# A graph network's message kernel: the first message product of the even quad moved ahead of the rank products

## The reference

```
msg  = concat(x[dst], edge_attr)            # 64 + 64 features per edge
h    = relu(msg @ W1a.T + b1a)              # 128 hidden
h    = h @ W1b.T + b1b                      # 64 per edge: the message
sums = segment_sum(h, src);  counts = segment_sum(1, src)
agg  = sums / max(counts, 1)
z    = relu(concat(x, agg) @ W2a.T + b2a) @ W2b.T + b2b
out  = concat(z, x) @ Wr.T + br
y    = layernorm(x + out)
```

## Time and profile before

| | us |
|---|---|
| median of three runs | 1564.77 |
| span of the profiled execution | 1564.5 |
| PE busy | 1519.9 (97%) |
| PE weight loads busy | 1241.7 (79%) |
| DVE busy | 1400.4 (90%) |
| ACT busy | 1042.4 (67%) |
| POOL busy | 1064.5 (68%) |
| mean granted TensorE clock | 0.990 |

### The profile page before, as it was taken

One profiled execution on the slowest core, in us unless ns is written; L12 is line 12 of the kernel. 1 busy time (PEld: TensorE's weight loads), 2 busy tenths in 40 slices (PEclk: granted clock), 3 DMA queues, 4 the chain that ended last, 5 costly groups with the idle time before them and its releaser, 6 DMA issues.

```text
span 1564.5 us, 42647 instructions
## 1 busy us (share of the span) xinstructions
PE 1519.9 (97%) x13326; PEld 1241.7 (79%) x13326; DVE 1400.4 (90%) x4356; ACT 1042.4 (67%) x2211; POOL 1064.5 (68%) x929
## 2 busy tenths in 40 slices
PE   8999999999999999999999999999999999996897
PEld 6678778778777877877878788888888888875786
DVE  5799999999999999999999999999999999885886
ACT  2587778778787787878877785665556665682222
POOL 2367767677676776767767777778777776876642
PEclk8999999999999999999999999999999999998999
DMA  7556656666565665656656669898999989768997
GB/s 208 166 164 162 177 158 166 170 166 166 159 177 163 164 175 159 167 164 171 165 157 175 174 170 314 261 292 290 294 275 292 293 271 286 230 192 266 367 370 238
DMA packets 135506, 335.44 MB, mean 214 GB/s; under 512 B 36506, under 2 KB 69565, under 8 KB 129016
## 3 DMA queue, kind: packets, MB, share of 16 engines
q0 software_dynamic: 53184, 224.62, 44.4%
q1 hardware_dynamic: 81028, 104.02, 26.3%
q10 hardware_dynamic: 1076, 4.09, 1.0%
HBM read 213.07 MB, written 119.52 MB: 213 GB/s over the span
## 4 chain that ended last, share of the span: by engine, by line
PE 82%; DVE 6%; DMA 3%; POOL 3%; issue 2%; ACT 2%; POOLq 0%; DVEq 0%; ACTq 0%
PE HH L556 21%; PE MS L565 19%; PE PA L581 12%; PE PBk L581 12%; PE RK L594 7%; DMA gbuf<-region,idx 3%; PE RK L674 2%; PE CK L641 2%; PE RK L679 2%; POOL region L1329 2%; PE PA L594 2%; DVE OH L1163 1%; DVE M L1042 1%; POOL gbuf L1357 1%; DVE pos L1047 1%
## 5 line engine op out<-in xcount | busy, mean ns | idle before, releaser
L1329 POOL DMA_INDIRECT region<-stg,dest x806 | 929.4, 1153 | 396.8 <-ACT stg L876 205.6
L565 PE MATMUL MS<-W,hT 128*128 128x64 f32 x3224 | 517.5, 261 | 3.7 <-issue 2.2
L565 PEld LDWEIGHTS MS<-W,hT 128*128 128x128 f32 x3224 | 467.6, 191 | 9.6 <-issue 5.5
L556 PE MATMUL HH<-eab,pw 128*128 128x512 f32 x806 | 433.6, 620 | 1.9 <-ACT hT L825 1.9
L1042 DVE TENSOR_SCALAR M<-pos_of,pos 128x384 bf16<-128x384 int16 x1612 | 427.8, 316 | 0.2
L581 PE MATMUL PA<-Z,M 128*128 128x195 bf16 x2418 | 338.1, 248 | 9.5 <-ACT stg L876 9.0
L581 PE MATMUL PBk<-Z,M 128*128 128x195 bf16 x2418 | 339.1, 248 | 0.0
L581 PEld LDWEIGHTS PA<-Z,M 128*128 128x128 bf16 x2418 | 224.0, 107 | 127.7 <-issue 119.6
L876 ACT ACTIVATE stg<-PA 120x585 bf16<-120x585 f32 x403 | 263.6, 654 | 91.7 <-PE PA L581 86.4
L825 ACT ACTIVATE hT<-HH 128x512 f32<-128x512 f32 x403 | 242.0, 600 | 84.3 <-PE HH L556 84.3
L876 ACT ACTIVATE stg<-PBk 120x585 bf16<-120x585 f32 x403 | 265.4, 659 | 46.2 <-PE PBk L581 44.3
(11 more groups left out here) (213 smaller groups left out, 1516.3 us busy)
## 6 DMA issues: line engine op xcount, KB each, us to landing
eab<-in_ea SPq DMA_DIRECT2D x201, 256.0 KB
kb<-keyd SPq DMA_DIRECT2D x201, 128.0 KB
pw<-ptab SPq DMA_DIRECT2D x403, 32.0 KB
region<-stg,dest POOLq DMA_INDIRECT x806
gbuf<-in_xt ACTq DMA_DIRECT2D x6, 422.5 KB
ptab<-OH SPq DMA_DIRECT2D x7, 256.0 KB, 2.6
gbuf<-region,idx POOLq DMA_INDIRECT x98, 8.7
eab<-in_xt SPq DMA_DIRECT2D x12, 130.0 KB
```

The source lines that it names most:

```text
L556: e.matmul(HH[:, :], pw[:, q % 4, :], eab[:, c % NB, at_q:at_q + GE], start=True, stop=True).then_inc(s_h, 1)
L565: ins = e.matmul(MS[:, o:o + D], hT[:, q % 2, 128 * j:128 * j + 128], W[:, W_1B:W_1B + D], start=True, stop=True)
L1329: e.indirect_dma_start(region[s], bass.IndirectOffsetOnAxis(ap=dest[:, g:g + 1], axis=0), stw[:, g % NS, :], None).then_inc(s_sc[g % NS], 16)
```

## The change

Message 0 of the even quad is issued directly behind `hidden(2m+1)`, ahead of `rank(2m)`. The other three stay in the second permutation, at new places: message 1 behind the fourth product of its first half (j = 1, t = 1), message 2 behind the first of its second half, message 3 behind the fifth. Where a turn has no permutation (the first one), messages 1 to 3 follow `rank(2m)` as before.

```diff
--- before.py
+++ after.py
@@ -584,8 +584,9 @@
                                                 start=t == 0, stop=t == 1)
                                 if (j, t) == (R - 1, 1):
                                     last.then_inc((s_pA, s_pB)[h], 1)
-                                if beside is not None and (j, t) in ((0, 1), (2, 0)):
-                                    message(beside, 2 * h + j // 2)
+                                beside_at = {(0, 1, 1): 1, (1, 0, 1): 2, (1, 2, 0): 3}.get((h, j, t))
+                                if beside is not None and beside_at is not None:
+                                    message(beside, beside_at)
@@ -735,6 +736,8 @@
                         if f is not None and 2 * f + 1 < NQ:
                             odd = 2 * f + 1
                             hidden(odd)
+                        if even is not None:
+                            message(even, 0)
                         if m < 0:
                             spin(e, HH, 4)
                         rank(2 * m)
@@ -742,7 +745,7 @@
                             permute(2 * m - 2, 0, even)
                             permute(2 * m - 2, 1, even)
                         elif even is not None:
-                            for j in range(4):
+                            for j in range(1, 4):
                                 message(even, j)
```

## The result

The changed kernel takes 1578.02 us (median of 6 runs, 1574.33 to 1584.55), the kernel before, run beside it, 1565.39 (median of 6). The ratio is 1.0073, with a 95% interval of 1.0052 to 1.0094: slower by 0.7%, as forecast. The forecast of 1578 us is met. With the forecast loss of 12.9 us added to the 1565.39 measured here it would be 1578.3.

A forecast was written before the change was run, and what follows sets the result against it. PE's own stream, busy 97% of the span, was taken as the bound, DVE close behind. First stage -2.9, regular class-sum turns +8.7, late turns +7.1 sum to +12.9 us: 1578 us, own range 1573 to 1582, 8 in 10 1571 to 1583.

The forecast's parts named there:

- The product's price: PE stream: a message costs 0.195 us among permutation products, 0.17 behind the odd first-layer product; the move saves 0.025 per turn.
- First stage: Main loop until 946 us: 117 of 144 turns gain 0.025 us each, 2.9 us in all; the other 27 gain nothing.
- The 0.01 of slack: Entry to `rank(2m+1)`, where message 0 of the odd quad waits for `pos`: slack 0.04 us, the 0.025 saving fits.
- The base of the sum: Profiled execution's 1564.5 us plus 12.9 gives 1577.4; the median 1564.77 lies 0.3 above, giving 1577.7, predicted as 1578.
- The wait moved forward: Second stage: message 0's wait on `rest` now stands ahead of the class sum; 38 regular turns lose 0.23 us each, 8.7.
- loop: Second stage: DVE and PE release each other in turn, 17.64 us per pair of turns against 17.18, +0.46 per pair.
- The late turns: Eight class-sum turns where DVE updates an index block or count chain before `rest`: +0.66 to 1.09 us each, together 7.1.
- the loop does not close: Rival, second stage: the wait is paid but DVE catches up in its gaps; +6 us, 1571; chance 12%.
- the queue goes round a waiting load: Rival: PE's queue passes message 0's wait, nothing is held up; 0.025 saved per turn, -4.3 us, 1560.5; chance 5%.
- The adds to T: Part of a rival: these adds gate `rank(2m+1)` and come too late, the 2.9 us is not gained; 1583; chance 8%.

The follow-up runs named there:

- experiment 1: Against the kernel before: message 0 early only in turns without a class sum, all four messages as before in the 46 class-sum turns; 1561.3 us, ratio 0.9963.
- experiment 4: Changed kernel, with DVE doing `rest` ahead of the `pos` and `dest` of the last rank in class-sum turns; 1564.93 us, ratio 0.9983 to the kernel before.
- experiment 5: Changed kernel with `rest` ahead of `pos` in class-sum turns, and message 0 back in the permutation in seven of the eight late turns; 1565.22 us, ratio 0.9984.
- experiment 7: Changed kernel, with message 0 directly behind the 30 class products in the 46 class-sum turns; 1563.8 us, ratio 0.9971 to the kernel before.
- experiment 3: Kernel before, with PE waiting for `rest` ahead of `rank(2m)` in the 46 class-sum turns, no message there (message 0 early in turn 0 alone); 1574.95 us, ratio 1.0056.
- experiment 8: Changed kernel plus one unused DVE copy (128x64) ahead of `rest` in each class-sum turn; 1582.03 us, ratio 1.0094 to the kernel before.
- experiment 2: Against the kernel before: message 0 early only in the 46 class-sum turns and turn 0; 1582.45 us, ratio 1.0096.
- experiment 11: Repeat, on another chip, of message 0 early only in turns without a class sum, against the kernel before; 1560.75 us, ratio 0.9962.

## Why the prediction was right

- **The product's price** (0.195 in the permutation, 0.17 behind the first-layer product): the plain turns measure a saving of 0.026; 0.025 was taken.
- **First stage**: -2.9 forecast, -3.9 measured, in the changed kernel and in experiments 1, 4, 5 and 7 alike. The 0.01 of slack at the entry of `rank(2m+1)` was enough. Of the 144 turns 103, not 117, are shorter by 0.02 to 0.035 us, together by 2.7. Five turns around the count chains (10, 41, 72, 103 and 134), which I had put at nothing, are shorter by 0.20 to 0.35 each, together by 1.2; why they are is not shown. The other 36 add up to nothing. This is the term that was mis-sized. The sum also left out the eight turns behind the class sums, which gain 0.5.
- **The base of the sum**: the prediction set the span of 1564.5 beside the median of 1564.77 and called them 0.3 apart. In every run on record with both numbers the execution's time is 1.9 us more than its span, so the profiled execution took about 1566.4. The forecast is the median plus 12.9 all the same, so it does not move.
- **The wait moved forward**: right in place, price and loop. The pair of turns came out at 17.61 against 17.64; experiments 3, 4, 7 and 8 each took one link of the loop away or added to it, and moved the regular turns the way the loop says (in experiment 3 the `dest` turns by 0.12 to 0.35, where 0.15 to 0.2 was expected). The 37 regular turns from 147 on are longer by 0.233 on average; 0.23 was forecast.
- **The late turns**: the one at 1110.77 was put at 10.05 us and is 10.02. The eight together were to cost 7.1 and cost 5.8; the difference is turn 146, which came out 0.6 shorter while turn 145 came out 1.7 longer. In both, ACT waits for the first gathers, and PE for ACT's evictions. In the kernel before PE's wait was in the second of the two:

```profile
955.15 0.26 ACT L855 ACTIVATE ids<-gbuf 128x60 bf16<-128x60 bf16 x1 [3.81 <-DMA gbuf<-region,idx]
...
956.10 0.67 PE L581 MATMUL PA<-Z,M 128*128 128x195 bf16 x6 [0.29 <-ACT stg L876]
```

  and in the changed one in the first:

```profile
943.78 0.26 ACT L858 ACTIVATE ids<-gbuf 128x60 bf16<-128x60 bf16 x1 [3.03 <-DMA gbuf<-region,idx]
...
944.73 0.68 PE L581 MATMUL PA<-Z,M 128*128 128x195 bf16 x6 [0.88 <-ACT stg L879]
```

  These two turns differ by up to 1.4 us between profiles of kernels with the same code there (turn 145 grows by 1.70 in the changed kernel and by 0.34 in experiment 2). The stage as a whole was put at 15.8 (8.7 + 7.1) and measured 16.1. That it came so near is in part luck: turns 145 and 146 hold +1.1 of it, in experiment 2 -0.2, where the stage is 14.8; the seven other late turns hold 6.4.
- **The rivals.** That the loop does not close is refuted by experiment 8: a copy of 0.10 us costs 0.10 us in nearly every regular turn. That the queue goes round a waiting load: the class products' first load begins 0.16 us or more behind the message's in every class-sum turn, and in experiment 3, behind the bare wait, 0.05 or more behind the end of `rest`. The Trainium skill's partial reorder window ("TensorE: Matmul & The Clock Gate", Architectural detail) shows here only as loads over a product in flight (641.05), not past a wait. The adds to T did not come too late: in no class-sum turn of the changed kernel did they release the first load of `rank(2m+1)`.

What was not tried: letting message 0 wait for the even quad's `rest` alone. Both halves of MS lie in one bank, which DVE would be reading while PE writes it, and no run here shows what that does. Left open are the 0 to 3 us between the sum of a kernel's turns and the shift of its median, most in experiments 2, 4 and 11; each sum is of one profile, and the start with turn 0 and the part behind the loop vary by 5.5 and 3.6 us from profile to profile.

## What to carry to other kernels

Before moving an instruction ahead in an in-order queue, list its waits and find when each ends in every stage of the kernel, not in the one where the gain is seen: here the wait had 0.8 us to spare in a plain turn of the first stage, 0.26 us too little in a `dest` turn of the second. Even in the first stage it ended last in seven turns near the count chains, where the load began 0.05 us behind `rest`; none of these seven gained. When two engines release each other, add up the loop between them, both parities if the turns alternate, and compare it with the bound engine's own turn; a move that makes the loop the longer one costs every turn. And apply such a move where it is free and leave it out where it is not: the loop is unrolled, so the condition costs nothing.

## What the runs showed of the hardware

- A float32 weight load under a 0.43 us pass added nothing to the stream (0.88 us from the first-layer product to what follows it, with a float32 or a bf16 load there), while between products of 0.083 us it shows with 0.026: that is what the plain turns save.
- Where PE stood waiting for DVE, its next load began 0.05 to 0.06 us after the recorded end of the DVE instruction: 503.27 to 503.32 in the old tight spot, 1045.59 to 1045.64 in the new one, 1046.96 to 1047.02 behind the bare wait of experiment 3.
- DVE's recorded durations overlap: a copy recorded at 0.18 us takes 0.10 in the stream. A sum of recorded durations overstates the time that DVE needs in a turn; the distance from start to start is to be used.
